# A graph network on one NeuronCore: the first scatter sent as 128 rows per indirect DMA, and ScalarE's first square root placed later in its staging loop

## The reference, cut to what matters

```python
e = edge_attr_16 @ We + be                                   # block 0
aggr = segment_sum(relu(h[src] + e), dst);  x += gelu((h + aggr) @ W1 + b1) @ W2 + b2
for _ in range(10): h = 0.9 * segment_sum(h[s] * wn, d) + 0.1 * feat_0      # block 1
...                                                          # block 2: three layers of edge attention
...                                                          # block 3: edge convolution
```

## Time and profile before

| | |
|---|---|
| median of 3 runs | 5552.65 us (5535.5 to 5559.93) |
| the profiled execution | 5549.77 us |
| its span, first to last instruction | 5547.7 us |
| POOL busy, share of the span | 3095.4 us, 56% |
| the 400 DMAs of the first scatter | 486.0 us busy, from 81.5 us |
| the 400 DMAs of the second scatter | 484.6 us busy |
| the 2080 gathers | 2094.5 us busy |

### The profile page before, as it was taken

The page is one execution under the profiler, slowest core; times in us unless marked ns, Lnnn a source line. Parts: engine busy times, 40 slices in busy tenths (PEclk is TensorE's granted clock), DMA queues, the critical chain, the costliest instruction groups (busy, mean ns, idle before and its releaser), DMA issues.

```text
span 5547.7 us, 80025 instructions
## 1 busy us (share of the span) xinstructions
PE 3415.8 (62%) x19963; PEld 2415.6 (44%) x19964; DVE 2805.2 (51%) x10030; ACT 935.2 (17%) x3274; POOL 3095.4 (56%) x3058
## 2 busy tenths in 40 slices
PE   2320068877789999756666466666466676344444
PEld 1310034444434444355556356656355665233333
DVE  7940078888721111355555555555555555533333
ACT  0000023333200000012111111112121222111111
POOL 3887766766688881155555345555355554355554
PEclk9999999999889999877666676667677767555555
DMA  4311133333599999511111211111211112011112
GB/s 138 89 22 9 13 94 81 81 77 79 112 332 358 359 356 364 191 41 43 42 42 43 43 40 42 42 42 43 43 44 42 43 44 39 19 20 20 18 19 21
DMA packets 295066, 498.24 MB, mean 90 GB/s; under 512 B 169771, under 2 KB 208300, under 8 KB 293434
## 3 DMA queue, kind: packets, MB, share of 16 engines
q1 hardware_dynamic: 119879, 339.99, 17.4%
q0 software_dynamic: 92160, 115.72, 11.9%
q10 hardware_dynamic: 82800, 40.01, 2.5%
HBM read 435.62 MB, written 58.97 MB: 89 GB/s over the span
## 4 chain that ended last, share of the span: by engine, by line
PE 40%; another core or an unknown queue 21%; DVE 13%; issue 12%; POOL 9%; ACT 2%; DMA 2%; DVEq 1%; SPq 0%; ACTq 0%; POOLq 0%
PE ps L1530 36%; POOL rows_dst L784 8%; DVE arena L1134 3%; PE ps L1766 2%; DVE arena L1133 2%; PE ps L1633 1%; DVE arena L1150 1%; DMA arena<-in_edge_attr_dram 1%; PE ps L1708 1%; DVE arena L1116 1%; DVE arena L1152 1%; DVE arena L1148 1%; ACT arena L1496 1%; DVE arena L1118 1%
## 5 line engine op out<-in xcount | busy, mean ns | idle before, releaser
L799 POOL DMA_INDIRECT arena<-table,arena x2080 | 2094.5, 1007 | 2099.0 <-DMA arena<-rows_dst 1185.1
L1530 PE MATMUL ps<-arena 128*128 128x96 f32 (+3 forms) x9176 | 1600.9, 360 | 539.0 <-issue 219.9
L1530 PEld LDWEIGHTS ps<-arena 128*128 128x128 f32 (+3 forms) x9176 | 1144.7, 213 | 903.4 <-issue 544.6
L1133 DVE TENSOR_SCALAR arena<-iota_row_b,arena 128x128 bf16<-128x128 bf16 x1664 | 434.9, 262 | 942.8 <-remote 786.6
L1633 PE MATMUL ps<-ident,arena 128*96 128x128 f32 x416 | 148.8, 358 | 977.3 <-ACT arena L1496 368.3
L1530 PE MATMUL ps<-arena,nodes 125*64 125x500 f32 (+2 forms) x3144 | 647.6, 536 | 27.3 <-DVEq L1225 16.6
L784 POOL DMA_INDIRECT rows_dst<-stage,arena x400 | 486.0, 1215 | 197.3 <-issue 121.6
L1134 DVE TENSOR_SCALAR arena<-iota_row_b,arena 128x128 f32<-128x128 bf16 x2080 | 573.1, 293 | 0.0
L757 POOL DMA_INDIRECT rows_src<-stage,stage_at x400 | 484.6, 1211 | 117.6 <-issue 111.1
L1633 PEld LDWEIGHTS ps<-ident,arena 128*96 128x96 f32 x416 | 68.8, 165 | 1039.2 <-issue 452.7
L1146 DVE TENSOR_TENSOR arena<-ps,arena 128x256 f32<-128x256 f32 x416 | 175.2, 421 | 527.9 <-remote 323.2
(11 more groups left out here) (286 smaller groups left out, 3777.1 us busy)
## 6 DMA issues: line engine op xcount, KB each, us to landing
arena<-dense SPq DMA_DIRECT2D x240, 750.0 KB
nodes<-dense SPq DMA_DIRECT2D x60, 750.0 KB
dense<-arena ACTq DMA_DIRECT2D x150, 250.0 KB
arena<-table,arena POOLq DMA_INDIRECT x2080
arena<-dense SPq DMA_DIRECT2D x60, 500.0 KB
arena<-rows_dst SPq DMA_DIRECT2D x208, 96.0 KB
arena<-dense SPq DMA_DIRECT2D x6, 2000.0 KB
arena<-pair_rows SPq DMA_DIRECT2D x12, 976.6 KB
```

Source lines behind the costliest of these rows:

```text
L799: nc.gpsimd.indirect_dma_start(rows[:, u, k, 0:width], None, frm, bass.IndirectOffsetOnAxis(ap=p[:, c, j, c_other:c_other + 1].bitcast(I32 ...
L1133: nc.vector.tensor_scalar(of(ohb, v_)[:, k, :], iota_row_b[:], key_at, None, ALU.is_equal)
L1530: return nc.tensor.matmul(to, lhsT, rhs, start=start, stop=stop, skip_group_check=True)
```

## The change

Three things change. The source tile `stage` gets 128 partitions instead of 125. The places get 128 partitions too (`pos_all`, whose first 125 partitions are the old `pos_dst`); an `iota` of POOL at the program's start fills it with row numbers behind the 128*416 real ones, so that partitions 125 to 127 of every DMA write to 1200 spare rows at the end of a longer HBM array. Each indirect DMA of the first scatter then takes 128 partitions. And ScalarE's square roots stand behind 46 staging groups instead of 25.

```diff
+ROOT_AT = 46
...
-        rows_dst = nc.dram_tensor("rows_dst", [128 * T, C], F32).ap()
+        rows_all = nc.dram_tensor("rows_dst", [128 * T + (128 - EP) * EJ, C], F32).ap()
+        rows_dst = rows_all[0:128 * T]
...
-        stage = sb("stage", [EP, 2, SG, C])
+        stage = sb("stage", [128, 2, SG, C])
...
-        pos_dst = carve([EP, EJ], I32)
+        pos_all = carve([128, EJ], I32)
+        pos_dst = pos_all[0:EP]
...
+            nc.gpsimd.iota(pos_all, [[1, EJ]], base=128 * T - EP * EJ, channel_multiplier=EJ)
...
                         nc.gpsimd.indirect_dma_start(
-                            rows_dst, bass.IndirectOffsetOnAxis(ap=pos_dst[:, j0 + j:j0 + j + 1], axis=0),
+                            rows_all, bass.IndirectOffsetOnAxis(ap=pos_all[:, j0 + j:j0 + j + 1], axis=0),
                             stage[:, h, j, :], None).then_inc(scattered[h], 16)
...
-            for q in range(G2):
+            for q in range(ROOT_AT):
                 stage_rows(q)
             root(rstd[:], var[:], 0)
...
-            for q in range(G2, 2 * G2):
+            for q in range(ROOT_AT, 2 * G2):
                 stage_rows(q)
```

More of the change, by code:

```diff
@@ L747, in prepare @@
                         if hi_c is None and lo_c == other:
-                            nc.gpsimd.tensor_copy(stage[:, h, :, lo_c].bitcast(I32), part[:, js])
+                            nc.gpsimd.tensor_copy(stage[0:EP, h, :, lo_c].bitcast(I32), part[:, js])
                         elif hi_c is None:
-                            nc.gpsimd.tensor_copy(stage[:, h, :, lo_c], part[:, js])
+                            nc.gpsimd.tensor_copy(stage[0:EP, h, :, lo_c], part[:, js])
                         else:
-                            nc.gpsimd.tensor_copy(stage[:, h, :, lo_c:hi_c], part[:, js, 0:hi_c - lo_c])
+                            nc.gpsimd.tensor_copy(stage[0:EP, h, :, lo_c:hi_c], part[:, js, 0:hi_c - lo_c])
                     nc.gpsimd.tensor_copy(stage_at[:, h, :], places[:, js]).then_inc(staged, 1)
@@ L758, in send @@
                             to, bass.IndirectOffsetOnAxis(ap=stage_at[:, h, j:j + 1], axis=0),
-                            stage[:, h, j, 0:width], None).then_inc(scattered[h], 16)
+                            stage[0:EP, h, j, 0:width], None).then_inc(scattered[h], 16)
                 def two_groups(i, first, last):
@@ L1383, in stage_rows @@
                     a.wait_ge(scattered[h], q // 2 * (16 * SG))
[L1384 to L1388, removed]
+                nc.scalar.copy(stage[0:EP, h, :, 0:DA], at16[:, js, :])
+                nc.scalar.copy(stage[0:EP, h, :, C_ATT3:C_ATT3 + DB], at3[:, js, :])
+                nc.scalar.copy(stage[0:EP, h, :, C_W], wgt[:, js])
+                nc.scalar.copy(stage[0:EP, h, :, C_KEY], lo[:, 1, js])
+                nc.scalar.copy(stage[0:EP, h, :, C_OTHER].bitcast(I32), key_i[:, 0, js]).then_inc(staged, 1)
             a.wait_ge(at_loaded, 16 * 2)
             a.wait_ge(at16_loaded, 16)
-            for q in range(G2):
+            for q in range(ROOT_AT):
                 stage_rows(q)
```

## The result

The changed kernel takes 5612.76 us (median of 4 runs, 5607.13 to 5621.01) where the kernel before takes 5555.54 us on the same chip: a ratio of 1.0114, 95% interval 1.0088 to 1.0141 (the two medians alone give 1.0103). It is slower by some 60 us; 5455 us was forecast. The profiled execution took 5621.01 us with a span of 5619.1 us, 71.4 us more than that of before.

The account below looks back on a forecast made before the run. POOL's price per scatter DMA, 400 times, was taken to set when message passing begins. 5549.8 - 97.2 + 0.5 = 5453 us, 5456 against the runs' median, written as 5455; range 5435 to 5475, 8 in 10 5425 to 5505.

Parts of the forecast that it names:

- The price: First scatter on POOL: each DMA falls from 1.190 to 0.947 us, stretch from 607.6 to 510.4, saving 97.2 us.
- Rivals 1, 2 and 3: Scatter price stays, 5550 to 5565, 10%; half the saving, 5504, 8%; slower from more pieces, 5810 at worst, 4%.
- rival 4: Scatter cheaper than the gathers, so SyncE waits last for `blk_ready`; 5415 us at 0.85 per DMA; 4%.
- Every 128-row DMA in this trace is cheap: Reading of the old trace: 128-row gathers have a median of 0.947 us, 125-row scatters 1.190.
- The iota: POOL's row-number fill at the start takes 0.42 us, ahead of the first staged group: +0.5 us.
- The places: VectorE finishes the last chunk at about 243 us, POOL wants it at about 552: no wait.
- the stretched 10.0 us: Scatter's busy time above 400 medians, from stretched instructions such as one beside a VectorE instruction; kept at 10.0 us.
- The staging: ScalarE stages a group in under 1 us while POOL takes 10 us for a group of 8: no wait.
- The square roots: ScalarE's roots follow the 46th group's staging at 531.8 us; `blk_ready` at 589.4, scatter landed at 593.9.
- The chain is still hidden, by about 4 us: Roots to `blk_ready`, 57.6 us, ends before the scatter's data lands; uncovered when a DMA, gap included, falls under 1.20.
- It follows as a block: Rest of the program after the scatter: what the scatter ends earlier or later, the end should too.
- Rival 3: Scatter slower because 16 pieces replace 5: up to 0.65 us per DMA, 5810 us at worst; 4%.

Follow-up runs that it names:

- e16: The changed kernel with a POOL memset of 312 elements ahead of each of the first 384 scatter transfers, distance 1.48 us; ratio 1.0012.
- e2: The changed kernel with 125 rows in every scatter transfer, root still behind group 46, spare rows not written; ratio 0.9987.
- e1: The changed kernel with the root back behind group 25, 128 rows kept; 5722.31 us, ratio 1.0185.
- e8: The changed kernel with 125 rows in scatter groups 0 to 24, 128 in groups 25 to 49, root behind group 25; ratio 0.997.
- e10: The changed kernel with only the first 25 rows of each column in every scatter transfer, 100 left out; 5671.9 us in one run.
- e4: The changed kernel with 384 of VectorE's 400 comparisons in loops of 8 instead of written out; 5720.49 us, ratio 1.0171.
- e11: The changed kernel with 128 rows only in scatter groups 25 to 45, 125 in the others, root behind group 25; ratio 0.9951.
- e13: e8's kernel with a POOL memset of 320 elements ahead of each of the first layer's first 32 gathers; 5513.26 us, ratio 0.9945.

## Why the prediction was wrong, point by point

**The price: right.** 0.958 us against the forecast 0.947, 388.3 us busy against 400 * 0.947 + 10.0 = 388.8. That the sum agrees so closely is luck: 400 * 0.958 = 383.2, so only 5.1 us were stretched, and the dearer median made up for it. The packets over 2 KB are gone, and line 761 stayed. Rivals 1, 2 and 3 are out, and so is rival 4's cause. One reading behind the forecast was wrong, "Every 128-row DMA in this trace is cheap": in the kernel before, the first layer's 416 gathers of 128 rows have a median of 1.177 us.

```profile
L799 POOL DMA_INDIRECT arena<-table,arena x416: 942/1177/2451, 706.4 to 1474.0; - x139
```

So 128 rows alone do not make the low price everywhere. In the scatter they did, with VectorE held (0.958) and with VectorE free (0.964 in e16).

**The iota: right**, 0.46 us, and e2 shows that it costs nothing that can be measured; for the spare rows e16 shows it.

**The places: this step failed.** I wrote "VectorE finishes chunk 2 of `placed` at about 108 and the last at about 243 ... No wait." These times were read from a trace in which transfers were 1.49 us apart and taken over into a kernel with 1.26 us. At 1.26 VectorE and TensorE are held, and the last chunk comes at 624. The same unspoken premise stands in the stretched 10.0 us, "VectorE does the same work afterwards": I looked at what VectorE does to POOL and not at what POOL does to VectorE. The traces of before could not have shown the hold in the scatter. They had transfers 1.25 us apart in the later gathers only, and I did not look at the other engines there. A look would have misled: in block 2, 29 gathers go out 1.26 us apart without a pause (their first and last are the two POOL lines), and 28 us into them VectorE, which had waited for 16.78 us, runs 15 instructions in 4 us (the first and last of them are shown), not held at all.

```profile
3143.17 0.94 POOL L799 DMA_INDIRECT arena<-table,arena  x1 [0.30 <-issue]
...
3178.46 0.95 POOL L799 DMA_INDIRECT arena<-table,arena  x1 [0.30 <-issue]
```
```profile
3171.25 0.42 DVE L1146 TENSOR_TENSOR arena<-ps,arena 128x256 f32<-128x256 f32 x1 [16.78 <-remote]
...
3175.12 0.27 DVE L1134 TENSOR_SCALAR arena<-iota_row_b,arena 128x128 f32<-128x128 bf16 x1
```

**The staging: right as far as it goes**; groups are staged in time except where the root stands.

**The square roots: failed as a consequence.** Group 46 was to be staged at 532 us and the root to follow; it was staged at 594, and the root waited until 690.8 for a variance that was to be ready at 320. "The chain is still hidden, by about 4 us" became 20.6 us in which SyncE waits for `blk_ready` alone; the chain from the root on took 66 us instead of 56. That is the shape of rival 4, an uncovered chain, from another cause: a late variance. Moving the root was still the better place: at 25 it costs 0.7% more (e1).

**"It follows as a block": true of the loss, only partly of the gain.** In the change, 66.5 us at the first gather are 71 at the end. In e8, 47 us at the first gather are 17 at the end.

Rival 3, slower because of more pieces, pointed the right way for a wrong reason: nothing costs POOL more.

**Open.** What the held engines wait for is not shown. It is not the shape of the transfers (e10, e16), not their rows or bytes (e10), and not written-out code alone (e4). The distance between transfers decides it within the scatter, but it is not enough by itself, as the gathers of block 2 show. Whether VectorE was free there because it had waited just before, or because of the kind of transfer or of its own instructions, no run tells. Nor do the runs tell the distance from the number of packets per time: whatever its rows, a transfer makes 32 packets on POOL's queue, 16 of them of 4 bytes. And every run here has its span from a profiler, so none shows whether the hold is there without one. The Trainium skill, "SBUF — State Buffer", section "Who interferes with whom", knows one port pair that VectorE and GpSimd share, and says that TensorE waits for nobody there. By that rule TensorE would run on; the trace has it at 6 to 9 matmuls in 20 us, from 104 in the kernel before, so this pair is not the account, or not the whole. It also stays open why the first gathers fall into the hold in e8 and e11 and not in before, and why e13 returns 30 us of 47; whether a longer scatter of another kind is held too was not tried.

## What to carry to other kernels

When an engine that feeds the DMA queues is made faster, its neighbours' times may not be taken over from the old trace: ask what each of them does while the faster engine works without pause, and look in the trace for a stretch in which that rate already occurs. Such a stretch can warn but not acquit: the one in block 2 showed no hold. A saving in a producer counts only where its consumers' inputs are long done; the same 0.23 us per transfer lost 60 us while places were still being computed, and gained 17 to 30 us behind that. A cheap way to tell rate from shape is to pace the new form down to the old rate: if the time is that of before, the form is innocent.

## What the runs showed of the hardware

- In the scatter, POOL's back-to-back indirect DMAs hold VectorE and TensorE: at 1.26 us apart VectorE gets through 15 to 19 instructions in 20 us instead of 119 and TensorE through 6 to 9 matmuls instead of 104. At 1.23 to 1.29 us apart the comparisons ended 331 to 364 us late, at 1.38 us 304 us late, and at 1.48 us or more not late at all. A pause of POOL of 12.55 us gave the two engines a stretch of nearly 20 us near full rate, as in the windows from 340 us. ScalarE's copies in the same stretches were not slowed (10 in 20 us, 1.43 us busy, as before). Gathers 1.26 us apart in block 2 did not hold VectorE.
- While held, VectorE's and TensorE's instructions start on a common grid. From 366 to 403 us their 51 starts all lie within 0.04 us of a grid of 0.70 us: VectorE at 372.46, 373.87, 375.95, 377.37 and, between them, TensorE:

```profile
374.57 0.20 PE L1532 MATMUL ps<-arena 32*125 32x25 f32 x1 [2.60 <-issue]
378.07 0.20 PE L1532 MATMUL ps<-arena 32*125 32x25 f32 x1 [3.30 <-issue]
```

  That looks like something shared by both, but no run here shows what.
- In the scatter, the price of an indirect DMA on POOL follows the rows in a piece, not the rows in all: 25 rows in pieces of 5 cost 0.923 us, 112 in pieces of 7 0.942, 128 in pieces of 8 0.958, 126 in pieces of 9 0.987, 125 in pieces of 25 1.187.
